# Output rows of the second scan turned on VectorE in 32x32 blocks and stored in 128-byte runs, in place of TensorE transposes, a ScalarE copy and 512-byte stores

## The reference

```
x = x + L0(_gn(x))      # group norm, then a 128x128 token mix (one matrix for each of 4 interleaved channel groups) + a bias per token
x = x + L1(_gn(x), W)   # group norm, then the scan below

def step(carry, row):                                   # over the 64 rows h
    new = row + jax.nn.relu(conv1d_same(carry, W))      # 9 taps along the 128 tokens, 64 -> 64 channels
    return (new, new)
```

## Time and profile before

| | us |
|---|---|
| median of 3 runs | 876.46 (875.48 to 876.52) |
| profiled execution, its own time | 875.68 |
| span of its trace | 873.6 |
| TensorE busy in the span | 799.9 (92%) |
| ScalarE / VectorE / GpSimd busy | 642.9 / 618.7 / 435.7 |
| DMA: moved in 203159 packets | 68.18 MB |

### The profile page before, as it was taken

The page is one execution under the profiler, slowest core; times in us unless marked ns, Lnnn a source line. Parts: engine busy times, 40 slices in busy tenths (PEclk is TensorE's granted clock), DMA queues, the critical chain, the costliest instruction groups (busy, mean ns, idle before and its releaser), DMA issues.

```text
span 873.6 us, 20141 instructions
## 1 busy us (share of the span) xinstructions
PE 799.9 (92%) x5734; PEld 732.1 (84%) x5734; DVE 618.7 (71%) x1536; ACT 642.9 (74%) x1462; POOL 435.7 (50%) x416
## 2 busy tenths in 40 slices
PE   1778887888799999999999999997999999999997
PEld 1555555555599999999899999997999999999997
DVE  7677778777578888989797978765555555555553
ACT  2477777777758887888788888887677677677664
POOL 1665655566265655566566665662333333333333
PEclk9999999999999999999999999999999999999999
DMA  9334343433134444444434343221222222223223
GB/s 186 68 74 96 74 96 72 90 78 83 38 74 93 90 97 98 98 90 94 90 84 91 87 96 74 49 50 37 62 62 67 66 60 67 65 60 68 64 60 72
DMA packets 203159, 68.18 MB, mean 78 GB/s; under 512 B 137556, under 2 KB 203092, under 8 KB 203092
## 3 DMA queue, kind: packets, MB, share of 16 engines
q1 hardware_dynamic: 203092, 67.43, 35.0%
HBM read 33.85 MB, written 33.55 MB: 77 GB/s over the span
## 4 chain that ended last, share of the span: by engine, by line
PE 71%; issue 9%; ACT 7%; DVE 7%; POOL 3%; ACTq 1%; DMA 1%; SPq 1%; DVEq 0%; POOLq 0%
PE ps_conv L898 30%; PE ps_conv L902 15%; PE ps_mix L812 8%; PE ps_mix L814 6%; PE ps_out L890 5%; ACT x_paired L424 5%; PE ps_in L827 5%; PE ps_small L801 2%; POOL xs L341 2%; POOL total L364 1%; DVE carry L732 1%; DVE x_sb L642 1%; DVE st L553 1%; DVE st L649 1%; DMA x_sb<-in_x_dram 1%
## 5 line engine op out<-in xcount | busy, mean ns | idle before, releaser
L364 POOL TENSOR_TENSOR total<-x_paired,carry 128x256 f32<-128x256 f32 x256 | 193.5, 757 | 299.6 <-DVE carry L732 293.5
L341 POOL TENSOR_TENSOR xs<-x_sb,rstd 128x512 f32<-128x512 f32 x128 | 232.9, 1846 | 93.6 <-DVE rstd L624 66.8
L424 ACT ACTIVATE x_paired<-ps_in,shift 64x256 f32 (+1 forms) x512 | 237.9, 465 | 7.8 <-POOL total L364 1.2
L740 DVE TENSOR_TENSOR carry_l<-carry,carry_h 128x256 fp32r<-128x256 f32 x252 | 177.0, 703 | 86.3 <-ACT carry_h L483 83.7
L898 PE MATMUL ps_conv<-carry_h,wh 128*128 128x256 f32 x1280 | 219.7, 303 | 4.7 <-ACT carry_h L483 4.7
L463 ACT ACTIVATE rows<-x_paired,shift,rstd 128x128 f32 (+1 forms) x512 | 221.3, 481 | 0.9 <-DVE shift L672 0.7
L483 ACT ACTIVATE carry_h<-carry 128x256 fp32r<-128x256 f32 x252 | 105.8, 420 | 140.9 <-DVE carry L732 139.0
L898 PE MATMUL ps_conv<-carry_h,wl 128*128 128x256 f32 x1280 | 197.7, 285 | 0.0
L902 PE MATMUL ps_conv<-carry_l,wh 128*128 128x256 f32 x1280 | 196.8, 284 | 0.0
L898 PEld LDWEIGHTS ps_conv<-carry_h,wh 128*128 128x128 f32 x1280 | 176.9, 192 | 7.2 <-ACT carry_h L483 5.6
L898 PEld LDWEIGHTS ps_conv<-carry_h,wl 128*128 128x128 f32 x1280 | 174.0, 190 | 0.0
(11 more groups left out here) (73 smaller groups left out, 354.9 us busy)
## 6 DMA issues: line engine op xcount, KB each, us to landing
x_sb<-in_x_dram SPq DMA_DIRECT2D x64, 512.0 KB, 4.0
out_dram<-staged SPq DMA_DIRECT2D x256, 128.0 KB, 2.4
x_paired<-in_L_conv_W_dram SPq DMA_DIRECT2D x2, 80.0 KB, 2.7
x_paired<-in_L_conv_W_dram SPq DMA_DIRECT2D x2, 64.0 KB, 2.4
x_paired<-v_attention_centers_dram SPq DMA_DIRECT2D x1, 0.0 KB
x_paired<-v_attention_spreads_dram SPq DMA_DIRECT2D x1, 0.0 KB
bias_col<-v_token_proj_n_bias_dram SPq DMA_DIRECT2D x1, 0.5 KB, 5.3
```

Source lines behind the costliest of these rows:

```text
L341: nc.gpsimd.tensor_tensor(xs[:, c % 2, heads, :, :], src, rstd1[:, m:G:2].unsqueeze(1).unsqueeze(1).to_broadcast([P, CG, CR, V]), ALU.mult ...
L364: nc.gpsimd.tensor_tensor(total[s][:, :].rearrange("p (w j) -> p w j", w=WS), x1_rows(wave, it, i, 1, s * WS, WS)[:, 0, :, :], carry[s][:, ...
L424: ins = nc.scalar.activation(dst[q * C:(q + 1) * C, r:HR:2, :], src[:, q, :, :], ACT.Identity, bias=shift1[r * C:(r + 1) * C, e:e + 1])
L740: nc.vector.tensor_tensor(carry_l[s][:, :, EDGE:EDGE + J], carry[s][:, :].rearrange("p (w j) -> p w j", w=WS), carry_h[s][:, :, EDGE:EDGE ...
```

## The change

In the second scan `turn_out` and `stage_out` are gone. VectorE gets `flip_out`, one instruction per half: it transposes each 32x32 block of `total[s]` by itself and writes into `staged`. Block (channel block, token-pair block) stays at its place; inside it channels and token pairs are exchanged. So a partition of `staged` now holds, for each image and each half of the token pairs, 32 channels of one token: a run of 128 bytes of the output. `store_flipped` stores a row by 8 DMAs (token parity x channel half x token-pair half), each 32 partitions x 8 images x 128 bytes. The first scan keeps the old path.

```
+    out_blocks = out.rearrange("b h (jh jl q) c -> b h jh jl q c", jl=BL, q=2)     # BL = 32
...
+            def store_flipped(h, buf):
+                rows_flipped = held(sp, h + 1)
+                alone(sp, w_zeroed)
+                for s in range(NS):
+                    sp.wait_ge(out_flipped[s], rows_flipped)
+                for q in range(2):
+                    for half in range(2):
+                        at = q * C + half * BL
+                        for jh in range(2):
+                            dst = out_blocks[W:B, bass.ds(h, 1), jh, :, q, half * BL:(half + 1) * BL]
+                            src = staged[at:at + BL, buf, :].rearrange("p (m jh c) -> p m jh c", jh=2, c=BL)
+                            sp.dma_start(dst.rearrange("m h j c -> (h j) m c"),
+                                         src[:, :, jh, :]).then_inc(flip_stored[buf], 16)
...
             def add_carry(wave, it, i, s):                       # GpSimd, before it writes total[s]
-                if not is_zero(t):
+                if wave == 0 and not is_zero(t):
                     pool.wait_ge(out_turned, t)
+                if wave == 1 and is_zero(it) and i == 0:
+                    pool.wait_ge(out_turned, t)
+                if wave == 1 and not (is_zero(it) and i == 0):
+                    pool.wait_ge(out_flipped[s], it * STEPS + i)
...
+            def flip_out(it, i, s):                              # VectorE
+                buf = (i + 1) % 2
+                h = it * STEPS + i - 1
+                if isinstance(h, int) and h < 2:
+                    dve.wait_ge(stored[buf], H // 2 * 32)
+                else:
+                    dve.wait_ge(flip_stored[buf], 128 * (it * (STEPS // 2) + (i - 1) // 2))
+                nc.vector.transpose(staged[:, buf, s * SW:(s + 1) * SW],
+                                    total[s][:, :]).then_inc(out_flipped[s], 1)
...
                             ALU.max, ALU.add).then_inc(carry_ready[s], 1)
+                        if wave == 1 and not (is_zero(it) and i == 0):
+                            flip_out(it, i, s)
...
-                        if s == 0 and not begins:
+                        if s == 0 and wave == 0 and not begins:
                             stage_out(t, (i + 1) % 2)
...
-                            if s == 0:
+                            if s == 0 and wave == 0:
                                 turn_out(t)
```

More of the change, by code:

```diff
@@ L51, in mix_and_scan_kernel @@
     x_nat = x.rearrange("b h n c -> n b h c")
+    BL = 32
+    out_blocks = out.rearrange("b h (jh jl q) c -> b h jh jl q c", jl=BL, q=2)
     out_pairs = out.rearrange("b h (j q) c -> b h j (q c)", q=2)
@@ L196, in mix_and_scan_kernel @@
         stored = [sem(f"stored{n}") for n in range(2)]
+        out_flipped = [sem(f"out_flipped{s}") for s in range(NS)]
+        flip_stored = [sem(f"flip_stored{n}") for n in range(2)]
         def x1_unit(wave, b, c, u):
@@ L278, in store_row @@
                                  src[e * J:(e + 1) * J, :, :]).then_inc(stored[buf], 16)
+            def store_flipped(h, buf):
[11 more added lines that the diff above has]
+                                         src[:, :, jh, :]).then_inc(flip_stored[buf], 16)
             def iteration(wave, it, b, e, more):
                 for i in range(STEPS):
-                    if not (is_zero(it) and i == 0):
+                    if wave == 1 and not (is_zero(it) and i == 0):
+                        store_flipped(it * STEPS + i - 1, (i + 1) % 2)
+                    if wave == 0 and not (is_zero(it) and i == 0):
                         store_row(wave, it * STEPS + i - 1, (it + wave * ITERS) * STEPS + i, (i + 1) % 2)
@@ L301, in _ @@
                 iteration(1, it, None, None, 0)
-            store_row(1, H - 1, 2 * H, 1)
+            store_flipped(H - 1, 1)
             for n in range(2):
-                sp.wait_ge(stored[n], 2 * H // 2 * 32)
+                sp.wait_ge(stored[n], H // 2 * 32)
+                sp.wait_ge(flip_stored[n], H // 2 * 128)
         @block.gpsimd
@@ L393, in _ @@
             rstd2_of(B - 1)
-            with pool.Fori(0, ITERS) as it:
+            iteration(1, 0, None, None, False, False)
+            with pool.Fori(1, ITERS) as it:
                 iteration(1, it, None, None, False, False)
@@ L530, in _ @@
             iteration(1, ITERS - 1, None, None, False, False)
-            stage_out(2 * H, 1)
         @block.vector
@@ L781, in _ @@
             finish(B - 1, 1, 1, W - 1)
-            with dve.Fori(0, ITERS - 1) as it:
+            iteration(1, 0, None, None, False, False)
+            with dve.Fori(1, ITERS - 1) as it:
                 iteration(1, it, None, None, False, False)
             iteration(1, ITERS - 1, None, None, False, False)
+            for s in range(NS):
+                dve.wait_ge(total_ready[s], 2 * H)
+                flip_out(ITERS, 0, s)
         @block.tensor
@@ L943, in _ @@
                 iteration(1, it, None, None, False, False)
-            turn_out(2 * H)
 _INS = ['x', 'L0_conv_attention_centers', 'L0_conv_attention_spreads', 'L0_conv_token_proj_n_bias', 'L1_conv_W']
```

## The result

The changed kernel takes 889.31 us in the median (887.88 to 889.41, 4 runs) against 875.97 (4 runs) for the kernel before: ratio 1.0148, 95% interval 1.0136 to 1.0161. It is slower by 13 us, 1.5%. Forecast were 1018 us and a range from 905. The direction and the place were right, the size was some ten times too large (142 us for 13).

The account below looks back on a forecast made before the run. SyncE's issuing of 8 store DMAs a row was to bind: 614.6 + 37.4 (first 7 rows) + 356 (56 loop rows) + 7.1 + 0.5 = 1015.6 us of span, 1018 us median; range 905 to 1085.

Parts of the forecast that it names:

- The bound moves to SyncE; everything else waits for it.: Second scan: 8 DMAs cost SyncE 6.30 us a row against TensorE's 3.64, so SyncE's queue never runs dry.
- The price of an issue: SyncE's 32-partition store was priced like the old 64-partition store: 0.603 us, pitch 0.787 in the loop, 0.667 outside.
- The address instruction, 0.184 us of each pitch.: In SyncE's loop, an address instruction between two store issues adds 0.184 us to each 0.603 us issue.
- The row's own 0.06 us.: Each SyncE loop row pays 0.06 us for its own register instruction, on top of 6.30 us.
- TensorE loses 0.45 us a row.: Second scan: dropping four transposes a row saves TensorE 0.45 us, 29 us over 64 rows, if it stays the bound.
- VectorE's transposes, 0.42 us, fit in the gap.: Each half's block transpose takes 0.42 us and fits VectorE's 0.48 us wait for ScalarE between the carry and `carry_l`.
- How the wait reaches the scan: A flip waits for the stores of the row two before; behind it queue `carry_l` and the other half's carry.
- The rule that speaks against the sum.: The skill calls DMA initiation usually small relative to the DMA; by that SyncE would not bind: 848 us.
- rival C: DMA engines bind: packets under 512 bytes cost two accesses, 68 ns, 8.65 us a row, 1173 us; with dearer issue, chance 0.14.
- Rival A: A small store issue costs SyncE only 0.23 us, pitch 0.414, so TensorE binds and the change gains: 848 us; chance 0.07.
- B: A store issue costs what x loads cost, 0.387 us, pitch 0.571: 909 us; chance 0.11 with what lies between 848 and 985.
- Rival D: TensorE's clock falls after 2.6 us idle a row, adding 0.1 to 0.6 us: 1025 to 1055 us; inside the forecast's 0.68.

Follow-up runs that it names:

- h1: Changed kernel with 4 of a row's 8 second-scan store DMAs, half of the token pairs never written: 847.12 us, ratio 0.9674.
- n4: Changed kernel with four buffers of `staged` instead of two, each with its own semaphore: 889.33 us, ratio 1.016.
- i1: Changed kernel with all 8 store DMAs of a row, each holding 4 of the 8 images, 128 packets instead of 256: 889.17 us, ratio 1.0152.
- b4: Kernel before, TensorE transposes kept, second-scan stores cut into 8 DMAs a row of 16 partitions x 4 images x 512 bytes: 890.0 us, ratio 1.0163.
- b1: Kernel before, second-scan stores cut by partitions into 4 DMAs a row of 32 partitions x 4 images x 512 bytes: 874.0 us, one run.
- b3: Kernel before, second-scan stores cut by images into 4 DMAs a row of 64 partitions x 2 images x 512 bytes: 876.2 us, one run.
- s1: Changed kernel with SyncE's loop over the second scan written out, so every store has a constant address: 875.09 us, ratio 0.9997 against the kernel before.
- q1: Changed kernel with 2 of a row's 8 store DMAs issued by ScalarE and 6 by SyncE, nothing left out: 849.17 us, ratio 0.9702.

## Why the prediction was wrong, point by point

- *The bound moves to SyncE; everything else waits for it.* Right: h1 takes the issues away and gets 847, n4 and i1 show that neither buffers nor data hold the row, b4 gets the slowdown from the number of DMAs alone.
- *The price of an issue: "I take 0.603, a pitch of 0.787 in the loop and 0.667 outside."* This is the step that failed. It was 0.316 and 0.50. I took the store as nearest because of its packets and its direction. Of what differs between the two (partitions, images, length of run), the partitions set the price, as b1 and b3 show. The error is 0.29 us x 8 x 56 = 129 us in the loop and 0.17 x 8 x 8 = 11 us outside, 140 together; less the 11 us by which the row's boundary was priced too low (next but one), that is the 129 us by which the sum missed. The sign was named beforehand ("an issue clearly off 0.603", 448 loop issues times the difference). The trace before had only 1, 64 and 128 partitions; a span from 0.414 to 1.0 of pitch was worked out, and 0.50 lay in it. Then the range was cut at 905 because I weighed the neighbours and not the gap between the bounds; 0.50 is next to the point of decision, 0.51, where I put a chance of 1%.
- *The address instruction, 0.184 us of each pitch.* Right for the loop, where 0.316 + 0.184 gives the 0.50 measured. But s1 shows that it is no saving to be had: 0.49 without it.
- *The row's own 0.06 us.* Too small: 0.25 us a row were measured in the loop, about 0.14 of them at every row's boundary and the rest in the loop's branch and long issues; 14 us went in s1. It is the term that turns "no change" (s1, 0.9997) into 1.5% slower.
- *TensorE loses 0.45 us a row.* Right: h1 and q1 return 28.5 and 26.5 us of the 28.8. *ScalarE's copy is worth nothing:* nothing contradicts it; it was not tried alone.
- *VectorE's transposes, 0.42 us, fit in the gap.* Right: 435 ns, and hidden in h1.
- *How the wait reaches the scan: the flip, then `carry_l` behind it.* Right, seen in the step above, in that order.
- *The rule that speaks against the sum.* The 16 packets that each DMA engine gets of one store take 16 x 11.9 ns = 0.19 us (worked out under rival C), and its pitch in the queue is 0.50. The rule of the Trainium skill ("DMA: Bandwidth & Descriptors", "Issuing engines are not separate DMA queues"), that initiating is usually small relative to the DMA, does not hold here by that measure. Against the whole way of a DMA it looks milder: the issue is 0.316 of the 1.5 us to landing. What binds is the pitch, and q1's second queue won 40 us.
- *Rival A* (pitch 0.414) and *B* (0.571): the truth lay between, nearer B in all three: an issue of 0.316 (0.23 and 0.387), a pitch of 0.50, a time of 889 (848 and 909). A's price rested on one 1x4 load of 0.23 us; the trace before holds another 1x4 load, of 0.35 us, which the prediction did not use:

```profile
0.76 0.35 SPq L246 DMA_DIRECT2D x_paired<-v_attention_centers_dram  x1
```

  B's way of pricing with the x loads, 909, was the best of the four.
- *Rival C*, DMA engines and packets under 512 bytes: refuted. In the second scan, 620 to 880 us, 132723 packets took 37.9% of 16 engines:

```profile
q1 hardware_dynamic: 132723, 16.02, 37.9%
```

  0.379 x 16 x 260 / 132723 = 11.9 ns for a 128-byte packet, a third of the 33.8 ns of a 512-byte one. A quarter of the bytes costs 0.35 of the time, not double. And i1, with half of the packets, takes the same time. The read-modify-write that the Trainium skill ("DMA: Bandwidth & Descriptors", "Specifications") names for runs under 512 B does not show in this time.
- *Rival D*, the clock: 0.99 in the stretch. TensorE stands still for 14.2 of 220 us, 0.27 us in a step of 4.25, and its longest wait from 660 to 880 us was 1.7 us, never 2.6. Nothing could be seen of D, since the idle time on which it rested did not come. For the same reason TensorE did not fall to 60% busy, a sign that the prediction named; it stayed at 94%.

## What to carry to other kernels

Count DMAs in a queue as one counts instructions on an engine: number per step x pitch, read from consecutive issues in the queue's own timeline, since no busy share on the page shows it. When a cheaper on-chip path splits a store into more DMAs, its gain stands or falls with that product against the step; here 6 + 2 over two queues makes a 3% gain out of a 1.5% loss. And where the price of a new shape is bounded from 0.4 to 1.0 and the decision falls at 0.51, the chances have to be spread over that span, not laid on the neighbour that looks most alike.

## What was not expected of the hardware

- In the loop an issue costs 316 ns for 16 or 32 partitions and 603 for 64, with every number of images and every run length tried; the x loads of 128 took 387 in the median, and up to 2726. For 32 partitions the pitch is 0.50 us with register instructions between (issue 316) and 0.49 without (issue 451). The four constant-address issues of a row in h1, where the queue had been idle, show how an issue lengthens (start, us):

```profile
618.12 0.32 SPq L296 DMA_DIRECT2D out_dram<-staged  x1
618.48 0.45 SPq L296 DMA_DIRECT2D out_dram<-staged  x1
618.98 0.46 SPq L296 DMA_DIRECT2D out_dram<-staged  x1
619.48 0.45 SPq L296 DMA_DIRECT2D out_dram<-staged  x1
```

  The first takes 0.32 us. The next starts 0.36 us later and takes 0.45, and from there on the pitch is 0.50. It looks as if something behind the instruction accepts one DMA in about 0.5 us; what that is, no run here shows.
- Landing differs too: 2.4 us after the issue begins for 64 x 4 x 512 bytes, 1.5 for 32 x 8 x 128.
- `carry_l` and `total` run at other speeds when the block transpose stands between them. `carry_l` before, then after, then `total` before and after (duration ns min/median/max, both from 650 us on):

```profile
L740 DVE TENSOR_TENSOR carry_l<-carry,carry_h x103: 707/716/768, 649.8 to 858.0; 128x256 fp32r<-128x256 f32 x103
...
L364 POOL TENSOR_TENSOR total<-x_paired,carry x104: 731/735/742, 649.5 to 860.0; 128x256 f32<-128x256 f32 x104
```

```profile
L779 DVE TENSOR_TENSOR carry_l<-carry,carry_h x105: 381/425/428, 650.7 to 872.0; 128x256 fp32r<-128x256 f32 x105
...
L390 POOL TENSOR_TENSOR total<-x_paired,carry x108: 722/800/922, 649.8 to 875.9; 128x256 f32<-128x256 f32 x108
```

  Before, GpSimd's `total` starts first (702.46) and `carry_l`, which starts into it at 702.71, takes 0.76 us. Now the transpose holds `total` back and `carry_l` starts first (702.03 in the step shown) and takes 0.38; `total` took 0.73 in that step and up to 0.92 in others. VectorE wins 0.29 us a half by that, more than half of what the transpose costs it. In h1, where VectorE does not wait for stores, the two are (650 to 840 us):

```profile
L779 DVE TENSOR_TENSOR carry_l<-carry,carry_h x103: 425/425/427, 650.9 to 836.2; 128x256 fp32r<-128x256 f32 x103
...
L390 POOL TENSOR_TENSOR total<-x_paired,carry x106: 721/910/981, 649.1 to 839.9; 128x256 f32<-128x256 f32 x106
```

  So it is not the waiting for stores that does it. That the order of the two is the cause fits the times but was not tested by itself.
